# Turning the attention outputs of two head groups at a time, and the query and key activation on ScalarE and GpSimd

## The reference

```
q, k, v = split(layernorm(x) @ w_qkv.T + b_qkv)         # 16 heads of 8 channels
q = elu(q) + 1 ; k = elu(k) + 1                         # before the rotation
q = rope(q) ; k = rope(k)
attn = softmax(q k^T / sqrt(8)) ; o = attn v            # per batch and head, 512 x 512
x = x + layernorm(o + depthwise_conv3(v) + b_lepe)
x = x + layernorm(moe(layernorm(x)))                    # 8 experts, top 2, and a shared one
```

## Time and profile before

| | us |
|---|---|
| median of three runs (lowest, highest) | 1276.27 (1275.63, 1276.97) |
| the profiled execution's own time | 1274.32 |
| its span, first to last instruction | 1272.4 |
| PE busy in the span | 1076.0 (85%) |
| DVE busy | 1075.7 (85%) |
| ACT busy | 948.7 (75%) |
| POOL busy | 854.7 (67%) |

### The profile page before, as it was taken

The page is one execution under the profiler, slowest core; times in us unless marked ns, Lnnn a source line. Parts: engine busy times, 40 slices in busy tenths (PEclk is TensorE's granted clock), DMA queues, the critical chain, the costliest instruction groups (busy, mean ns, idle before and its releaser), DMA issues. The chain is left out here.

```text
span 1272.4 us, 22262 instructions
## 1 busy us (share of the span) xinstructions
PE 1076.0 (85%) x6504; PEld 463.7 (36%) x6504; DVE 1075.7 (85%) x2480; ACT 948.7 (75%) x1752; POOL 854.7 (67%) x1134
## 2 busy tenths in 40 slices
PE   1499999999999999999999999898899999888900
PEld 0112222222322322223223232232677778666600
DVE  2398899999999999999999999972786888999944
ACT  1118888888888888888788888788788888777612
POOL 5445466676678887887878878553555645888675
PEclk9559999999999999999999999999899999988855
DMA  2553432423523334325234234103134644445322
GB/s 67 118 125 130 98 80 67 110 74 75 118 78 102 89 107 110 100 72 126 78 102 102 85 94 103 46 17 125 37 98 141 210 132 139 138 144 150 100 62 80
DMA packets 108985, 128.22 MB, mean 101 GB/s; under 512 B 14225, under 2 KB 81845, under 8 KB 108597
## 3 DMA queue, kind: packets, MB, share of 16 engines
q1 hardware_dynamic: 98848, 105.94, 30.7%
q0 software_dynamic: 8192, 16.79, 4.9%
q10 hardware_dynamic: 1824, 4.06, 0.9%
HBM read 58.85 MB, written 59.51 MB: 93 GB/s over the span
## 5 line engine op out<-in xcount | busy, mean ns | idle before, releaser
L1077 DVE TENSOR_REDUCE MX<-psS 128x1 f32<-128x512 f32 x1024 | 649.8, 679 | 62.6 <-PE psS L757 56.9
L972 ACT ACTIVATE PR<-psST 128x512 f32<-128x512 f32 x986 | 535.5, 599 | 113.2 <-PE psST L745 112.2
L757 PE MATMUL psS<-KS,QS 48*128 48x512 bf16 x1024 | 366.0, 400 | 36.0 <-DMA KS<-scratch_parts 23.7
L745 PE MATMUL psST<-QS,KS 51*128 51x512 bf16 x986 | 336.5, 385 | 37.8 <-ACT PR L972 21.6
L771 PE MATMUL psPV<-PR,V 128*32 128x512 f32 x2048 | 273.2, 605 | 7.8 <-ACT SHARED L886 1.5
L745 PEld LDWEIGHTS psST<-QS,KS 51*128 51x128 bf16 x986 | 78.8, 93 | 389.5 <-ACT PR L972 373.1
L1968 POOL DMA_INDIRECT SHARED<-scratch_y,FROM x128 | 130.7, 1021 | 43.6 <-issue 35.3
L462 POOL DMA_INDIRECT scratch_x<-XN,POSI x128 | 130.8, 1022 | 36.3 <-issue 33.5
L757 PEld LDWEIGHTS psS<-KS,QS 48*128 48x128 bf16 x1024 | 87.5, 93 | 90.7 <-DVE MX L1077 60.8
L1506 PE MATMUL psH<-XH,WS 128*128 128x512 f32 x164 | 73.8, 450 | 1.8 <-ACT XH L1598 0.8
L771 PEld LDWEIGHTS psPV<-PR,V 128*32 128x32 f32 x2048 | 40.8, 108 | 80.7 <-issue 61.7
(11 more groups left out here) (213 smaller groups left out, 1958.4 us busy)
## 6 DMA issues: line engine op xcount, KB each, us to landing
scratch_parts<-PT SPq DMA_DIRECT2D x192, 128.0 KB, 2.4
QS<-scratch_parts SPq DMA_DIRECT2D x64, 192.0 KB, 3.6
KS<-scratch_parts SPq DMA_DIRECT2D x64, 192.0 KB, 4.6
XR<-scratch_x SPq DMA_DIRECT2D x46, 256.0 KB, 2.8
scratch_y<-YR SPq DMA_DIRECT2D x46, 256.0 KB, 2.1
RES<-EL SPq DMA_DIRECT2D x64, 128.0 KB, 2.0
scratch_x<-ZERO SPq DMA_DIRECT2D x18, 256.0 KB
X<-in_x SPq DMA_DIRECT2D x16, 256.0 KB, 5.1
```

What stands on the lines that cost most here:

```text
L745: nc.tensor.matmul(bank(st_banks(t), k)[:], KS[t.par][rows, h // 2, kc * P:(kc + 1) * P], QS[t.par][rows, h // 2, :], start=True, stop=Tru ...
L757: nc.tensor.matmul(bank(psS, k)[:], QS[b.par][rows, h // 2, qc * P:(qc + 1) * P], KS[b.par][rows, h // 2, :], start=True, stop=True).then_ ...
L972: nc.scalar.activation(PR[:, s % 2, j, :], bank(st_banks(t), k)[:], ACT.Exp, scale=SCALE).then_inc(st_exp, 1)
L1077: nc.vector.tensor_reduce(out=MX[:, qc, h:h + 1], in_=bank(psS, k)[:], axis=AX.X, op=ALU.max).then_inc(s_max, 1)
```

## The change

Two things are changed, and waits and bank lists follow.

Turning: `turn_heads` now takes two groups at once. In place of four transposes of 128 columns for each group (16 in a pass) it issues eight matrix products for each pair of groups (16 in a pass), with the same copy in OT as the stationary operand and 36 chosen columns of the identity (`PICKED`, nine of every 32) as the moving operand. Groups 0 and 1 are turned in slot 10, groups 2 and 3 in slot 4 of the next pass; the turns in slots 7 and 14 are gone. `copy_heads` for group 0, in slot 4, now waits for the turn of slot 4, since it overwrites the buffer that this turn reads. DVE normalises twice in a pass, with twice the elements.

Activation: after each L907, ACT computes relu(projection + bias) into EL; POOL, after its minimum, adds EXQ to EL. DVE's `elu` is gone. The convolution taps stay where they were. Two waits are added on DVE ahead of the statistics of batch t+3, on work of the pass before.

```diff
-    def turn_heads(self, pe, b, g, m):
+    def turn_heads(self, pe, b, hf, m):
         nc = self.nc
-        pe.wait_ge(self.ot_ready, b.done(4, g + 1))
+        pe.wait_ge(self.ot_ready, b.done(4, 2 * hf + 2))
+        wide = HG * (D + 1)
         for qc in range(QC):
-            last = nc.tensor.transpose(m[:, qc * P:(qc + 1) * P], self.OT[:, g % 2, qc * P:(qc + 1) * P], self.IDF[:])
+            for g in range(2):
+                at = wide * (2 * qc + g)
+                last = nc.tensor.matmul(m[:, at:at + wide], self.OT[:, g, qc * P:(qc + 1) * P], self.PICKED,
+                                        start=True, stop=True)
...
-        MISC = ["xT", "q", "k", "mT1", "O3", "O0", "lepeT", "mT0", "O1", "vT", "xT2", "V",
-                "O2", "lg"]
+        MISC = ["xT", "q", "k", "mT1", "O23", "lepeT", "mT0", "O01", "vT", "xT2", "V", "lg"]
...
-                if due(before := b.done(4, g - 1)):
+                if due(before := b.done(2, g // 2)):
                     act.wait_ge(oT_psum, before)
                 nc.scalar.activation(OT[:, g % 2, :], psPV[:], ACT.Copy).then_inc(ot_ready, 1)
...
                     nc.scalar.activation(EXQ[:, w, :], misc_bank("qk"[w])[:], ACT.Exp,
                                          bias=CHAN[:, w:w + 1]).then_inc(qk_exp[w], 1)
+                    if due(before := prep.done(1, 0)):
+                        act.wait_ge(rot_cos[w], before)
+                        act.wait_ge(turned[w], 32 * before)
+                    nc.scalar.activation(EL[:, w, :], misc_bank("qk"[w])[:], ACT.Relu,
+                                         bias=CHAN[:, w:w + 1]).then_inc(qk_linear[w], 1)
...
-                nc.vector.scalar_tensor_tensor(out=EL[:, w, :], in0=misc_bank("qk"[w])[:], scalar=BP1[:, w:w + 1],
-                                               in1=EXQ[:, w, :], op0=ALU.add, op1=ALU.max).then_inc(qk_elu[w], 1)
...
                 nc.gpsimd.tensor_scalar(EXQ[:, w, :], EXQ[:, w, :], 1.0, -BIG, ALU.min, ALU.max).then_inc(qk_min[w], 1)
+                pool.wait_ge(qk_min[w], b.done(1, 1))
+                pool.wait_ge(qk_linear[w], b.done(1, 1))
+                nc.gpsimd.tensor_tensor(EL[:, w, :], EL[:, w, :], EXQ[:, w, :], ALU.add).then_inc(qk_elu[w], 1)
```

More of the change, by code:

```diff
@@ L142, in __init__ @@
         self.xtl_loaded = [sem(f"xtl_loaded{i}") for i in range(2)]
-        self.REC = sb("REC", [P, QC, HG], F32)
+        self.REC = sb("REC", [P, QC, HALF], F32)
+        self.PICKED = IDF[:].rearrange("p (j v) -> p j v", v=VW)[:, :, 0:D + 1]
         self.NHALF = sb("NHALF", [P, QC], F32)
@@ L246, in store_turned, with normalise @@
         sp.dma_start(self.XTD[b.number()], self.XT2[:, b.par, :]).then_inc(self.xT2_stored[b.par], 16)
-    def normalise(self, dve, b, g, bank):
+    def normalise(self, dve, b, hf, bank):
         nc = self.nc
-        m = bank[:].rearrange("p (q j v) -> p q j v", q=QC, j=HG)
-        dve.wait_ge(self.oT_psum, b.done(4, g + 1))
-        if due(before := b.done(4, g)):
+        m = bank[:, 0:QC * HALF * (D + 1)].rearrange("p (q j v) -> p q j v", q=QC, j=HALF)
+        dve.wait_ge(self.oT_psum, b.done(2, hf + 1))
+        if due(before := b.done(2, hf)):
             dve.wait_ge(self.o_norm, before)
         nc.vector.reciprocal(self.REC[:], m[:, :, :, D]).then_inc(self.recip, 1)
-        dve.wait_ge(self.recip, b.done(4, g + 1))
-        if g == 0:
+        dve.wait_ge(self.recip, b.done(2, hf + 1))
+        if hf == 0:
             if due(before := b.done(1, -1)):
                 dve.wait_ge(self.z_ready, before)
-        y = self.Y[:, b.par, :, g * HG * D:(g + 1) * HG * D].rearrange("p q (j d) -> p q j d", j=HG)
-        nc.vector.tensor_tensor(y, m[:, :, :, 0:D], self.REC[:].unsqueeze(3).to_broadcast([P, QC, HG, D]),
+        y = self.Y[:, b.par, :, hf * HALF * D:(hf + 1) * HALF * D].rearrange("p q (j d) -> p q j d", j=HALF)
+        nc.vector.tensor_tensor(y, m[:, :, :, 0:D], self.REC[:].unsqueeze(3).to_broadcast([P, QC, HALF, D]),
                                 ALU.mult).then_inc(self.o_norm, 1)
@@ L529, in attention @@
         qk_min = [sem(f"qk_min{w}") for w in range(2)]
+        qk_linear = [sem(f"qk_linear{w}") for w in range(2)]
         qk_elu = [sem(f"qk_elu{w}") for w in range(2)]
@@ L793, in misc @@
                 if s == 4 and prev.live:
[L794 to L798, removed]
+                    misc_freed(pe, t, "O23")
+                    ends.turn_heads(pe, prev, 1, misc_bank("O23"))
                 if s == 8 and prev.live:
@@ L805, in misc @@
                 if s == 10 and t.live:
-                    misc_freed(pe, t, "O1")
-                    ends.turn_heads(pe, t, 1, misc_bank("O1"))
+                    misc_freed(pe, t, "O01")
+                    ends.turn_heads(pe, t, 0, misc_bank("O01"))
                 if s == 11 and nxt.live:
@@ L819, in misc @@
                     last.then_inc(v_psum, 1)
-                if s == 14 and t.live:
-                    misc_freed(pe, t, "O2")
-                    ends.turn_heads(pe, t, 2, misc_bank("O2"))
                 old = t + (-2)
@@ L991, in _ @@
             dve.wait_ge(ones_set, 1)
[L993 to L999, removed]
-                nc.vector.scalar_tensor_tensor(out=EL[:, w, :], in0=misc_bank("qk"[w])[:], scalar=BP1[:, w:w + 1],
-                                               in1=EXQ[:, w, :], op0=ALU.add, op1=ALU.max).then_inc(qk_elu[w], 1)
             def extra(t, s, j):
                 nxt, prep, prev, far = t + 1, t + 2, t + (-1), t + 3
-                if s in (2, 3) and j == 3 and prep.live:
-                    elu(prep, s - 2)
                 if s == 5 and j == 3 and prev.live:
-                    ends.normalise(dve, prev, 3, misc_bank("O3"))
-                if s == 8 and j == 1 and t.live:
-                    ends.normalise(dve, t, 0, misc_bank("O0"))
+                    ends.normalise(dve, prev, 1, misc_bank("O23"))
                 if s == 9 and j == 1 and prev.live:
@@ L1014, in extra @@
                 if s == 11 and j == 1 and t.live:
-                    ends.normalise(dve, t, 1, misc_bank("O1"))
-                if s == 15 and j == 1 and t.live:
-                    ends.normalise(dve, t, 2, misc_bank("O2"))
+                    ends.normalise(dve, t, 0, misc_bank("O01"))
                 if s == 10 and j == 1 and prev.live:
@@ L1025, in extra @@
                     dve.wait_ge(x_loaded[far.par], far.done_par(16))
+                    if due(before := far.done(1, 0)):
+                        dve.wait_ge(aggr0, before)
                     for qc in range(QC):
@@ L1030, in extra @@
                     dve.wait_ge(stats0, far.done(1, 1))
+                    if due(before := far.done(1, 0)):
+                        dve.wait_ge(xn_ready, before)
                     dve.sem_inc(passed, 1)
@@ L1533, in drain @@
                 if p == 0:
-                    pe.wait_ge(ends.o_norm, last.done(4, 4))
+                    pe.wait_ge(ends.o_norm, last.done(2, 2))
                     ends.turn_lepe(pe, last, psG)
@@ L1561, in drain @@
                     turn_gates(QC - 1, psG)
-            ends.turn_heads(pe, Batch(B - 1), 3, psG)
+            ends.turn_heads(pe, Batch(B - 1), 1, psG)
             take(0)
@@ L1855, in _ @@
             turn(0)
-            ends.normalise(dve, Batch(B - 1), 3, psG)
+            ends.normalise(dve, Batch(B - 1), 1, psG)
             for p in range(END):
```

12 lines of the change are left out of this document (5 added, 7 removed).

## The result

The changed kernel takes 1309.74 us (median of four runs, 1301.21 to 1316.64) against 1276.62 (four runs, 1275.63 to 1277.93): 1.0256 times as long, with a 95% interval of 1.019 to 1.0322. The forecast was 1311. The profiled execution is the fastest of its four, 1301.21 us, 26.9 above the 1274.32 of the profiled one before. So two things have to be explained: 27 us that the traces show side by side, and the 6 more between the medians.

A forecast was written before the change was run, and what follows sets the result against it. The prediction took a loop between PE and ACT as the bound. Terms 13.5 + 7.0 + 13.3 + 1.9 + 0.4 - 1.5 = +34.6 us on 1274.3 gave 1308.9, with the median 2 higher 1311; range 1288 to 1327.

The forecast's parts named there:

- Which loop leads: Attention block: a loop between PE and ACT sets the pace; DVE mostly follows, leading only in gate passes.
- Price of a product, 0.24: Turning: each 36-column float32 product takes 0.24 us, 1.92 a turn of eight; bounds 0.148 and 0.31 each.
- four-times rule: Turning: float32 transpose mode is four times faster, so eight products cost 2.25 times the old four, 1.33 us a turn.
- LDWEIGHTS (loading the stationary operand): Turning: a load costs its 128 columns however few move, about 107 ns; two loads each, 1.7 us a turn.
- Slot 4, +13.5: Slot 4: longer turn delays ACT's copy of group 0 and the next values, +0.9 us in 15 passes, +13.5.
- Slot 10, +7.0: Slot 10: longer turn delays the projection of v by 0.7 us, in nine plain passes and the last, +7.0.
- Relu, +13.3: ACT: two relus a pass add 1.18 us, 0.95 after waits, in 14 passes, +13.3; bounds 6.7 and 16.5.
- Slots 7 and 14, nothing: Slots 7 and 14: removed turns, 0.59 us each, gain nothing because the fourth exponential ends last.
- DVE, -1.5: DVE: 2.3 us less work a pass, worth about 0.3 in each of five gate passes, -1.5 us.
- Prologue, +1.9: Pass -2: two POOL adds with gaps, 2.8 less a 0.98 wait, push transfers and PE's first scores by 1.9 us.
- POOL, +0.4: POOL's chain to the rotation: the adds cost 0.1 us in four passes and otherwise hide beside relu and turn.

The follow-up runs named there:

- gap version: Kernel before, with six kinds of ACT jobs moved from a slot's end to behind the next slot's second exponential: 1308.73 us against 1317.57, ratio 0.9927; repeated 0.9935.
- the relu in the gap: Changed kernel, each relu moved from behind the projection's exponential to behind the second exponential of the next slot: 1313.11 us, 1.0319 times the kernel before.
- the new activation on the gap version: Gap version with relu on ACT behind the next slot's second exponential, add on POOL, no elu, turning as before: 1326.33 us, 1.0084 times the kernel before.
- the one with three copies: Changed kernel with a third buffer for OT, so the copy of group 0 overwrites nothing slot 4's turn reads: 1344.29 us, one run on the slower chip.

## Why the prediction was right, term by term

- *Which loop leads.* Right. DVE's work fell by 24 us and no plain pass became shorter; DVE's waits for PE rose to 119 us, PE's for DVE fell to 5.0, not quite "near zero". The gap version shows the same from the other side: DVE's work is as before and the plain passes are a microsecond shorter.
- *Price of a product, 0.24.* Right: 0.239 measured, between 0.235 at 8 columns and 0.241 at 64. The Trainium skill's four-times rule ("TensorE: Matmul & The Clock Gate", section "Terms"), with its estimate of 1.33 us a turn, does not hold against the measured 1.91. The Trainium skill's rule in the same page's section "LDWEIGHTS (loading the stationary operand)", an estimate of 1.7 us, came nearer; the trace has a load at 191 ns, above its 107.
- *Slot 4, +13.5.* Measured: 0.80 in the passes where slot 4 had been 3.46, 0.66 in those where it had been 3.60, 1.2 in the last three (3.05 before): 12.7. The copy's wait is shown to be on the path, but it is the smaller part: without it 0.28 of the 0.80 goes, and 0.52 is PE's own.
- *Slot 10, +7.0.* Measured 0.70 over slots 10 and 11 in each of nine plain passes, about 8 with the last two.
- *Relu, +13.3.* Measured 0.96 in 14 passes, 13.4. In the gap it is 0.68 less.
- *Slots 7 and 14, nothing.* Nearly: slots 14 and 15 of the plain passes lost 0.2, some 1.6 us that I had not counted.
- *DVE, -1.5.* The mechanism was right, the size not: in the gate passes slots 8 to 11 fell from 14.58 to 13.54, 1.04 each in four of them, while pass 4 became 0.1 longer: 4.0 less in all. I had put down 0.3 a pass, though the earlier trace rows had 11.1 us of PE waiting for DVE; 6 of them went.
- *Prologue, +1.9.* Mis-sized. (Two adds with their gaps, 2.82, less 0.98 are 1.84, so 1.8 on its own terms.) PE's first scores came at 48.54, 0.9 later, since the first minimum lay 0.3 earlier and the transfers absorbed another 0.5. The first values came only 0.25 later, though pass 0 then lost 1.0 in its first slot. That 1.0 goes with the clock: PE came to its full clock later in this execution, as the rows of the values and of the next scores show (before, then after). It is not tied to the edits: that slot varies from 3.6 to 4.6 us over the traces, and took 4.27 in the first trace of the gap version, which has neither edit.

```profile
48.54 1.03 PE L760 MATMUL psS<-KS,QS 48*128 48x512 bf16 x3 [24.80 <-DMA KS<-scratch_parts]
```

```profile
97.84 1.51 PE L771 MATMUL psPV<-PR,V 128*32 128x512 f32 x8
99.28 0.39 PE L745 MATMUL psST<-QS,KS 51*128 51x512 bf16 x1
```

```profile
98.09 1.94 PE L774 MATMUL psPV<-PR,V 128*32 128x512 f32 x8
99.95 0.60 PE L748 MATMUL psST<-QS,KS 51*128 51x512 bf16 x1
```

- *POOL, +0.4.* Right that POOL hides here, and only in this kernel. (2.0 less 1.85 in four passes is 0.6, not 0.4.) The wait for ROT is 20.2 us, as it was before (19.2), with single waits like the 0.58 us in pass 8, where the earlier trace rows have 0.52.

The sum was +34.6. The traces have +28.8 up to the last values and 26.9 for the whole: DVE's relief is 2.5 us more than forecast, slots 14 and 15 give 1.6, slot 4, POOL, and the prologue with the first slot of pass 0 are some 2 less, slots 10 and 11 are 1 more, and 2 us go behind the block. The median still came out at 1310, 6 us above what the first trace has. The second profiled execution lost as much at the lower clock, which no step of the prediction had; that the executions without a trace did too is likely and not shown. The DVE term, too small, and the missing clock worked against each other in the median, so the 1.3 us between forecast and median is luck; the working was 7.7 us off, 34.6 against 26.9. Three of my later expectations (the activation alone, the relu in the gap, and the new activation on the gap version) failed for one reason: their theories priced ACT's loop, while POOL's chain runs beside it and was late. Each of the three had that as a rival.

## What to carry to other kernels

Find the loop that leads and price an edit by the place where it enters that loop: the same relu costs 0.96 us a pass behind the last exponential of a slot and 0.3 behind the second. A second chain with little slack (here POOL's) belongs in the sum, and its slack changes with every edit to the first; so parts of a change that are tested alone need not add up to the whole. For plain float32 products of 8 to 64 columns count the products, not the columns: here 0.24 us each.

## What the runs showed of the hardware

- A plain float32 product holds PE for 0.235, 0.239 and 0.241 us at 8, 36 and 64 moving columns (the profile has two loads and two products for each); a transpose of 128 columns took 0.148 in one record.
- In 11 of the 14 traces the granted clock fell to 0.50 (1.2 GHz) in the middle of the attention block, for 3 to 14 us at a time; in the traces of the kernel before, of the changed kernel's first execution and of the one with three copies it did not before the last pass. It happened behind the 8-column turn of slot 4 in eight of 15 passes, and behind slot 10 in seven of 16 when that turn stood there, which ties it to the turn (one execution each). It also followed waits of PE: with the activation alone, in nine of nine passes behind a wait of 1.5 us (1.0 in the first of them); with the relu in the gap, in the four gate passes behind waits of 1.6 us and in none of the five plain ones behind waits of 0.9 to 1.1; with the new activation on the gap version, behind one of 1.35 us and not behind two of 1.46. What decides whether it falls in a given pass was not settled. It may be what widens the spread: the changed kernel ran from 1301 to 1317 us on chips where the one before stayed between 1274 and 1278.
- Before the first values PE ran at its lower clock in either kernel: a score product of 512 columns takes 0.60 us there and 0.39 later. The profile's clock column says 0.50 for the kernel before and 1.00 for the changed one from 40 to 96 us, but the rows of the changed one contradict that, as the one below does. The clock's first entry in that trace is at 101.2 us, and the column gives 1.00 where there is none. So it pays to check a granted clock against the length of a product that is known, and the mean clocks of whole executions (0.936 and 0.967) can't be compared.

```profile
95.50 0.60 PE L748 MATMUL psST<-QS,KS 51*128 51x512 bf16 x1
```

- On the chip of the later eight experiments what follows the last values took 422 to 431 us in place of 386 to 392, whichever kernel. For the changed kernel PE's busy time there was 306 us against 293 in its first trace, and DVE's 304 in both, so most of it was waiting. In the eight traces from that chip the profile names "remote" as what ended 74 to 141 us of the engines' waits in all, and of none in the six others; what that was, was not settled. The last pass of the attention block is longer there too, by 5 to 9 us.
